# Two softmax types of a differential attention in two 64-row halves of the TensorE array

## What is computed

```python
Q = split_heads(X @ W_q.T); K = split_heads(X @ W_k.T); V = split_heads(X @ W_v.T)   # 16 heads of 2*8
Q1, Q2 = (Q[..., :dh], Q[..., dh:])                    # dh = 8
K1, K2 = (K[..., :dh], K[..., dh:])
A1 = where(causal, einsum('bhqd,bhkd->bhqk', Q1, K1) * scaling, -inf)
A2 = where(causal, einsum('bhqd,bhkd->bhqk', Q2, K2) * scaling, -inf)
attn = softmax(A1, -1) - lam * softmax(A2, -1)
O = einsum('bhqk,bhkd->bhqd', attn, V)                 # then a norm over the 16 values of a head, and W_o
```

## Time and profile before

| | |
|---|---|
| median of three runs | 1586.29 us |
| the profiled execution, and its span | 1589.78 us, 1588.0 us |
| TensorE busy, of the span | 1366.6 us, 86% |
| TensorE weight loads | 1063.3 us, 67% |
| VectorE | 1180.9 us, 74% |
| ScalarE | 885.0 us, 56% |
| GpSimd | 868.0 us, 55% |
| mean granted TensorE clock | 0.954 |

### The profile page before, as it was taken

How to read it: one execution, slowest core, us unless ns; L and a number is a source line. 1 busy time by engine, 2 the same in 40 slices (tenths; PEclk the granted TensorE clock), 3 DMA queues, 4 the chain that set the end, 5 groups by cost and what they waited for, 6 DMA issues and landing times. The chain is left out here.

```text
span 1588.0 us, 42685 instructions
## 1 busy us (share of the span) xinstructions
PE 1366.6 (86%) x13344; PEld 1063.3 (67%) x13345; DVE 1180.9 (74%) x3082; ACT 885.0 (56%) x1918; POOL 868.0 (55%) x1279
## 2 busy tenths in 40 slices
PE   1499999999999999999999999962599999999950
PEld 1266777767777776777777676641588888888850
DVE  4567888888888888788888887866666666666647
ACT  1166777777777777777777777652133333333310
POOL 2045577677767767676776776663233333333334
PEclk9999999999999999999999999985799999999985
DMA  6433443444344354444434533300211111111139
GB/s 213 123 100 83 129 118 94 118 118 114 103 126 121 92 133 110 103 110 118 122 88 120 128 98 90 87 24 14 59 48 43 46 43 42 46 43 45 42 94 295
DMA packets 176591, 152.61 MB, mean 96 GB/s; under 512 B 21491, under 2 KB 159097, under 8 KB 176036
## 3 DMA queue, kind: packets, MB, share of 16 engines
q1 hardware_dynamic: 159096, 123.07, 30.1%
q0 software_dynamic: 8448, 16.93, 3.3%
q10 hardware_dynamic: 8880, 10.49, 1.9%
HBM read 89.37 MB, written 61.55 MB: 95 GB/s over the span
## 5 line engine op out<-in xcount | busy, mean ns | idle before, releaser
L988 ACT ACTIVATE probs<-p_exp 128x512 f32<-128x512 f32 x768 | 446.5, 603 | 183.6 <-PE p_exp L812 164.3
L1402 POOL TENSOR_SCALAR_AFFINE_SELECT probs<-probs 128x256 f32<-128x256 f32 (+1 forms) x768 | 365.4, 485 | 286.4 <-ACT probs L988 278.3
L1166 DVE TENSOR_REDUCE mx<-p_max 128x2 f32<-128x512 f32 x512 | 351.4, 687 | 169.9 <-PE p_max L786 168.9
L647 POOL DMA_INDIRECT pair_out<-on,v x136 | 133.6, 982 | 284.7 <-ACT on L557 279.3
L784 PE MATMUL p_max<-kt,qt 96*128 96x256 bf16 x1024 | 198.6, 275 | 40.5 <-DMA kt<-k_parts 19.7
L835 PE MATMUL p_out<-probs,v 128*32 128x256 f32 (+1 forms) x4096 | 221.0, 333 | 14.0 <-POOL probs L1402 7.5
L812 PE MATMUL p_exp<-qt,kt 100*128 100x256 bf16 x1024 | 196.7, 273 | 16.8 <-DMA qt<-max_parts 14.0
L621 DVE TENSOR_TENSOR ot<-ot,p_max 128x512 f32<-128x512 f32 x136 | 93.5, 688 | 125.8 <-PE p_max L508 106.5
L1169 DVE TENSOR_REDUCE mx<-p_max 128x4 f32<-128x512 f32 x256 | 173.2, 676 | 2.1 <-PE p_max L795 2.0
L835 PEld LDWEIGHTS p_out<-probs,v 128*32 128x32 f32 x4096 | 112.4, 109 | 85.4 <-POOL probs L1402 24.4
L1449 POOL DMA_INDIRECT rows_sorted<-h,idx x128 | 137.4, 1074 | 50.7 <-ACT probs L988 28.6
(11 more groups left out here) (169 smaller groups left out, 2757.9 us busy)
## 6 DMA issues: line engine op xcount, KB each, us to landing
qt<-q_parts SPq DMA_DIRECT2D x64, 384.0 KB
q_parts<-part_h SPq DMA_DIRECT2D x96, 128.0 KB, 2.0
kt<-k_parts SPq DMA_DIRECT2D x128, 96.0 KB
v<-rows_sorted SPq DMA_DIRECT2D x136, 65.0 KB, 1.8
q_parts<-part_m SPq DMA_DIRECT2D x64, 128.0 KB, 2.0
kt<-k_parts SPq DMA_DIRECT2D x128, 64.0 KB
qt<-pair_out SPq DMA_DIRECT2D x32, 256.0 KB, 5.4
mods<-mod_rows SPq DMA_DIRECT2D x32, 192.0 KB
```

Source lines behind the costliest of these rows:

```text
L647: nc.gpsimd.indirect_dma_start(pair_out, bass.IndirectOffsetOnAxis(rows_in[:, j.slot, DIM:DIM + 1].bitcast(U32), 0), rows_out[:, j.slot, : ...
L988: nc.scalar.activation(probs[:, g % 2, k, :], p_exp[:, k, :], ACT.Exp, scale=SCALE).then_inc(exp_done.sem, 1)
L1166: m = V.reduce_max(mx[:, w, 1, :, h8:h8 + 1].rearrange("p t o -> p (t o)"), p_max[:, bank, :].rearrange("p (t k) -> p t k", t=2), AX.X, ne ...
L1402: G.affine_select(out=blocks, in_=blocks, compare_op=ALU.is_ge, fill=zero, base=0, pattern=[[0, 2 if k < 2 else 4], [1, P]], channel_multi ...
```

## The change

`qt` and `kt` are laid out anew. Rows 0 to 51 belong to type 0 and rows 64 to 115 to type 1, and `kt` has one copy. In each half stand 48 rows of parts, two edge rows and two rows for the maxima. A score product of one type then uses 64 rows of the array (a lane), and the other lane is left for another product.

A bank holds one type. Of four heads (a quad), units k = 0 to 3 are two heads' queries 128 to 255 of one type, and units 4 and 5 four heads' queries 0 to 127. The type alternates from unit to unit, and `scores` issues the products of the maxima of type t and those of the exponentials of type 1 - t in turn.

The mask has two parts. The edge rows add -1e30 to the keys of the upper half of a 128 x 128 block for the queries of its lower half, inside the score product itself. The two remaining 64 x 64 triangles are added by two products of 64 rows with `tri4`. Other things that move:

- `outputs` of a quad come together, both pairs in slots 2, 6, 10 and 14 (before: one pair in each odd slot), and the copies of `p_out` one slot later (slots 3, 7, 11 and 15 for 2, 6, 10 and 14).
- `probs` has six banks a quad instead of three a pair. The first transposition of outputs goes from slot 11 to 12.
- Queries are loaded in two DMAs of 48 rows instead of one of 96; maxima are saved in two and loaded in two. The maxima are turned in one product of 128 columns instead of two of 32.
- At the start, the memset of `kt` on GpSimd goes, eight loads of edge rows come, and TensorE alone waits for them and for the ones, not VectorE. The experts' low weights and tables lie in other tiles (`qt`, `probs`).

```diff
+LANE = 64
+QK_ROWS = SLOTS * DH
+EDGES = 2
+SHIFT_AT = QK_ROWS + EDGES
+ALL_ROWS = SHIFT_AT + SHIFTS
...
+        def unit_heads(n):
+            k, h = n % 6, n // 6 % 2 * 4
+            return range(h + 2 * (k // 2), h + 2 * (k // 2) + 2) if k < 4 else range(h, h + 4)
...
-                sp.dma_start(qt[0:QK_ROWS, slot, :, :],
-                             q_parts[bass.ds(b.n, 1), :, :, :, w * HU:(w + 1) * HU, :]
-                             .rearrange("a t s d h k -> (a t s d) h k")).then_inc(unit_loaded[w].sem, 16)
                 for t in range(2):
+                    sp.dma_start(qt[LANE * t:LANE * t + QK_ROWS, slot, :, :],
+                                 q_parts[bass.ds(b.n, 1), t, :, :, w * HU:(w + 1) * HU, :]
+                                 .rearrange("a s d h k -> (a s d) h k")).then_inc(unit_loaded[w].sem, 16)
...
+                for tile in range(NT):
+                    sp.dma_start(max_parts[bass.ds(b.n, 1), w, :, :, :, tile * P:(tile + 1) * P]
+                                 .rearrange("a t s h k -> (a t s h) k"),
+                                 nmt[tile * rows:(tile + 1) * rows, w, :]).then_inc(nm_saved.sem, 16)
+                wait(sp, nm_saved, b, 16 * NT * (w + 1))
+                for t in range(2):
+                    at = LANE * t + SHIFT_AT
+                    sp.dma_start(qt[at:at + SHIFTS, 2 * b.par + w, :, :],
+                                 max_parts[bass.ds(b.n, 1), w, t].rearrange("a s h k -> (a s) h k")
+                                 ).then_inc(nm_loaded[w].sem, 16)
...
+            def max_unit(b, n):
+                t, k, bank, slot, heads = n % 2, n % 6, n % 2, 2 * b.par + n // (NBANKS // 2), unit_heads(n)
+                rows = slice(LANE * t, LANE * t + SHIFT_AT)
+                masks = slice(LANE * t, LANE * t + LANE)
...
+                for j, h in enumerate(heads):
+                    if k < 4:
+                        yield nc.tensor.matmul(p_max[:, bank, j * SEQ:(j + 1) * SEQ], qt[rows, slot, h, P:SEQ],
+                                               kt[rows, slot, h, :], start=(j == 0), stop=False)
...
+                for half in range(2):
+                    c = (P if k < 4 else 0) + LANE * half
+                    m = nc.tensor.matmul(blocks[:, :, c:c + LANE], (idb if half == t else ids)[masks, :],
+                                         tri4[masks, 0:len(heads), :], start=False, stop=(half == 1))
...
+            def exp_unit(b, n):
+                t, k, bank, slot, heads = 1 - n % 2, n % 6, n % 3, 2 * b.par + n // (NBANKS // 2), unit_heads(n)
+                rows = slice(LANE * t, LANE * t + ALL_ROWS)
...
+            def scores(bm, be, n):
+                for _ in itertools.zip_longest(max_unit(bm, n), exp_unit(be, n)):
+                    pass
```

More of the change, by code:

```diff
@@ L3 @@
 from contextlib import ExitStack
+import itertools
 import numpy as np
@@ L746, in move_max @@
                 wait(sp, nmt_ready, b, w + 1)
[L747 to L752, removed]
+                rows = NM_COLS // NT
+                for tile in range(NT):
[3 more added lines that the diff above has]
+                wait(sp, nm_saved, b, 16 * NT * (w + 1))
+                for t in range(2):
+                    at = LANE * t + SHIFT_AT
+                    sp.dma_start(qt[at:at + SHIFTS, 2 * b.par + w, :, :],
+                                 max_parts[bass.ds(b.n, 1), w, t].rearrange("a s h k -> (a s) h k")
+                                 ).then_inc(nm_loaded[w].sem, 16)
             iterations(sp, body, looped=False)
@@ L770, in _ @@
             pe.wait_ge(setup_a, 2)
-            def scores_for_max(b, h, n, rows):
-                w, h8, bank = h // HU, h % HU, n % 2
-                slot = 2 * b.par + w
+            pe.wait_ge(edges_loaded, 16 * EDGE_LOADS)
+            def max_unit(b, n):
+                if not active(b):
+                    return
+                t, k, bank, slot, heads = n % 2, n % 6, n % 2, 2 * b.par + n // (NBANKS // 2), unit_heads(n)
+                rows = slice(LANE * t, LANE * t + SHIFT_AT)
+                masks = slice(LANE * t, LANE * t + LANE)
                 if n in (0, NBANKS // 2):
-                    wait(pe, unit_loaded[w], b)
+                    wait(pe, unit_loaded[n // (NBANKS // 2)], b)
                 if n >= 2:
@@ L781, in scores_for_max @@
                     wait(pe, max_done, b.plus(-1), NBANKS - 1 + n)
[L782 to L796, removed]
@@ new lines, in max_unit @@
+                blocks = p_max[:, bank, :].rearrange("p (j k) -> p j k", j=len(heads))
+                for half in range(2):
+                    c = (P if k < 4 else 0) + LANE * half
+                    m = nc.tensor.matmul(blocks[:, :, c:c + LANE], (idb if half == t else ids)[masks, :],
+                                         tri4[masks, 0:len(heads), :], start=False, stop=(half == 1))
+                    if half == 1:
+                        m.then_inc(max_ps.sem, 1)
+                    yield m
@@ L1157, in _, with take_max @@
             assert count[0] == SETUP_DONE
-            def take_max(b, h, n, rows):
-                w, h8, bank = h // HU, h % HU, n % 2
+            def take_max(b, n):
+                w, t, tile, bank, heads = n // (NBANKS // 2), n % 2, int(n % 6 < 4), n % 2, unit_heads(n)
                 wait(dve, max_ps, b, n + 1)
```

182 lines of the change are left out of this document (93 added, 89 removed).

## The result

The changed kernel takes 1767.6 us, median of four runs (1761.2 to 1795.9), against 1587.5 of the kernel before; the ratio is 1.113 (95% 1.108 to 1.118). The slowest of the four ran in a second, slower state at a lower granted clock, and the ratio leaves it out. I had said 1610, with a range to 1643: slower, as forecast, but by 180 us instead of 24. The profiled execution has a span of 1766.6 us against 1588.0.

A forecast was written before the change was run, and what follows sets the result against it. The bound was taken to be a closed ring per round, engines (15.6 us) then SyncE and DMA (15.1). Ring + 22.5, clock + 5, setup - 4 on 1589.8 gave 1613, at the median 1610; range 1574 to 1643.

The forecast's parts named there:

- the ring over SyncE: The loop's round, engine work then SyncE's saves and DMA: + 0.75 us per round, + 22.5 over 30 rounds.
- TensorE's round falls by some 3.7 us: TensorE per round: side-by-side lanes save 5.2 us, more changes of array shape cost 1.5.
- Part A, + 0.15: First exponential scores to first save, 15.6 us, set by the engines: + 0.15, between - 0.5 and + 1.4.
- Part B, + 0.6: First save to next round's first exponential scores, 15.1 us, SyncE and DMA: + 0.6, bounds + 0.28 and + 0.94.
- E0: The moment of a round's first exponential scores, held 16 times by the maxima's DMA, 18.9 us in all.
- The round is a closed ring: nothing outside A and B can shorten it: Claim that Part A plus Part B, 30.7 us, make up the whole round of 30.8.
- The clock, + 5: TensorE waits longer at E0, its clock drops: 1.2 us in each of four more rounds, + 5.
- rival four: TensorE's clock falls in every round behind a held E0: + 54.5, 1641 us; chance 0.12.
- Setup, - 4: At the start, VectorE's wait and kt's memset go, ten small loads precede x: - 4, between - 6 and + 6.
- rival three: TensorE's two row lanes run one after the other: + 56, 1642 us; chance 0.10.
- Faster rival: TensorE is the bound after all, the round falls to 29.4 us: 1543 us; chance 0.14.

The follow-up runs named there:

- e9: e6 with the two saves of the first unit's maxima issued before SyncE waits for the parts to land: 1582.9 us, 0.996.
- e6: e5 with extra TensorE products (16 before unit 15, 6 behind unit 0) and the ten small edge loads on ScalarE's queue: 1624.6 us, 1.025.
- e1: The changed kernel with a quad's two output blocks in two slots instead of both in one: 1677.4 us, 1.058.
- e5: e1 with ScalarE's slot 15 copies of p_out behind the normalized rows xn and h2 instead of ahead of them: 1632.4 us, 1.027.
- e10: e9 without the extra products on TensorE: 1609.2 us, 1.012.
- e13: e2 with the same 26 extra products per round over 128 rows instead of 52: 1686.0 us, 1.062.
- e14: e9 with 10 extra products over 128 rows per round instead of 22 narrow ones: 1578.8 us, 0.994.
- e11: The kernel before the change, with its one save of the maxima ahead of SyncE's wait for the parts: 1582.8 us, 0.994.
- e3: The changed kernel with the edits of e1 and e2 together: 1668.3 us, 1.050.
- m1: Not the layer's kernel: TensorE products over 128 rows, 50 rows in one lane or 50 in two, without and with pauses; clock 0.50 over 50 rows back to back.
- e2: The changed kernel with extra products on TensorE, 16 before unit 15 and 10 behind unit 0: 1714.1 us, 1.079.
- e4: The changed kernel with a unit's maxima products issued first and the exponentials behind them, instead of alternating: 1792.8 us, 1.129.

## Why the prediction was wrong

Direction right, size wrong by 157 us. The direction was luck: the term that made my sum positive, the ring over SyncE, didn't bind in the changed kernel, where the first exponential scores stood behind the maxima's DMA 3 times and not in every round. Step by step:

- **TensorE's round falls by some 3.7 us**: the total is right. In e9, at full clock, TensorE is busy 28.3 us of a 31 us stretch; 22 extra products at 0.11 are 2.4 of it, so 25.9 against 29.65. One piece was too dear: two tall units start at 525.74 and have issued all by 526.36, about 0.33 us each, not 0.55. The estimate that I had set aside from Part 3 of "TensorE: Matmul & The Clock Gate" of the Trainium skill, 0.44, was the nearer one. So eight tall units took 1.8 us less than I had counted, something else took as much more, and no run says what: the total is right by some luck.
- **Part A, + 0.15**: wrong on either side. The copies moved behind two exponentials as I had said, but the second part_h stood at 528.73, 11.4 us behind the first exponential scores (517.29) instead of 9.95. All of the difference arose ahead of the copies, where 519 to 522 ran at half pace and both output blocks stood in slot 2. A was 17.1. In a round of e6 at full clock the second part_h came 8.9 us behind these scores (599.11 and 590.24), and A was 14.6 (590.24 to 604.81): below my lower bound.
- **Part B, + 0.6**: 16.7 in that round of e6 (573.53 to 590.24), + 1.6, above my bound of + 0.94. I had taken the 3.2 us from the save of the maxima to their load as they were and thought that they might hide the further issues; with two saves they grew to 4.6 there, and to 4.0 in the changed kernel (509.71 to 513.73). Why is open. In the changed kernel B was 17.9, but the engines, not the DMA, set it: no wait at E0. "The round is a closed ring: nothing outside A and B can shorten it" fitted the kernel before, and it is the failed step: I moved the ring by 0.75, where the mean round grew by 5.9, and did not ask what the engines do inside A and B when TensorE is no longer the one that comes last.
- **Not seen at all: both output blocks in one slot.** I noted that they move, priced ScalarE's copies, and not that 1.5 us without new scores starve VectorE, which has two banks of scores, and ScalarE, which has three. e1: 90 us, a part of which may be the clock.
- **Not seen: the copies in slot 15 in front of xn.** I followed the same move in slot 3 only. e5: 45 us.
- **The clock, + 5**: the mechanism was named, the place and the size were not. I looked for waits at E0; the falls came behind other waits, before unit 15 and behind unit 0, at least twice a round. The sign that I had given for rival four, a clock under 1.00 in every stretch, came true when a stretch is a round. And I did not know that 50-row products hold the clock less well. Rival four ("the clock falls in every round") priced a round's fall at 1.2 us, where some 7 to 14 us of a round ran at half pace; e9 against e10 gives 26 us with the rest mended, e13 against the changed kernel 82 with it not.
- **Setup, - 4**: wrong sign. VectorE's wait for the ones did go, but x, the real end of setup, stands behind ten loads: about + 9 by the second save. The run-out behind the last first save grew by 11.5 us, a term that I didn't have.
- **The lanes run in turn**, rival three: refuted, they start 0.01 us apart, and the kernels without the overlap are 136 and 201 us slower.
- Faster rival: not reached. Even mended (e14, 0.994) the change is worth no more than e11's edit alone (0.994). That VectorE, 26 us busy in a round, stands right behind TensorE is the likely reason; no run tests it.

The chain from 1768 to 1579 us: outputs split - 90, xn first - 45, edge loads and early save of the maxima - 23, the clock kept by ten wide products - 30. These steps were taken in this order; e3 shows that they overlap, so each is its worth in this row only. The kernel before, run beside each of them, moved by up to 7 us meanwhile; by the ratios the last two steps are 24 and 29 us.

## What to carry to other kernels

When a change frees a dense engine, list every in-order wait that this engine has behind others; there it will stand next, and its clock may fall there. Ask of every block that a change merges how long the consumers' buffers last while it runs, and follow every instruction that it moves in each slot in which it occurs. Halving the rows of TensorE's products is no free move even where the column time is the same: here it made the clock fragile (m1, and e13 against e2).

## What the runs showed of the hardware

- Products over 50 rows in one lane, TensorE 100% busy for 66 us: granted clock 0.50; over 128 rows, or in two lanes of 50 at once, busy without a pause: 1.00 (m1).
- With pauses of 1.4 us one lane of 50 rows stayed at 0.50 for all of 90 us, two lanes for about 50 us, and 128 rows did not fall once they were at 1.00 (m1). In the kernel 26 products per round over 128 instead of 52 rows were worth 28 us (e13 against e2).
- A product of the other row lane starts beside the first of four that stand ahead of it in TensorE's list (e4: 501.82 and 501.84).
- Extra work made a kernel faster: 26 discarded products per round, 53 us (e2), 82 when they are wide.
